# Joining the first feed-forward block and attention of a macaron layer into one program, with batch 0's norm, weight split and projections inside the last feed-forward group

## The reference, cut to what matters

```python
x = x + 0.5 * ffn(layernorm(x), w_gate, w_up, w_down)      # x: (8, 512, 512) float32
x = x + attention(layernorm(x), w_q, w_kv, w_proj, b_proj)
x = x + 0.5 * ffn(layernorm(x), w_gate, w_up, w_down)
# ffn: h = silu(x @ w_gate) * (x @ w_up)   (2048 wide); of each 4 neighbours of h the two of largest
#      size are kept, the others set to 0; then h @ w_down
# attention: 16 heads of 32; one k and one v head shared by all; rotary with xpos scales on q and k;
#      causal softmax; @ w_proj.T + b_proj
```

## Time and profile before

| | us |
|---|---|
| median of 3 runs | 2837.68 |
| lowest, highest | 2837.28, 2841.86 |
| the profiled execution, its own time | 2843.29 |
| its span in the trace | 2841.4 |
| TensorE busy over the span | 2738.1 (96%) |
| VectorE, ScalarE, GpSimd busy | 1863.3, 1127.3, 284.3 |
| mean granted TensorE clock | 0.984 |

### The profile page before, as it was taken

One profiled execution on the slowest core, in us unless ns is written; L12 is line 12 of the kernel. 1 busy time (PEld: TensorE's weight loads), 2 busy tenths in 40 slices (PEclk: granted clock), 3 DMA queues, 4 the chain that ended last, 5 costly groups with the idle time before them and its releaser, 6 DMA issues. The chain is left out here.

```text
span 2841.4 us, 41676 instructions
## 1 busy us (share of the span) xinstructions
PE 2738.1 (96%) x15520; PEld 2198.9 (77%) x15520; DVE 1863.3 (66%) x3543; ACT 1127.3 (40%) x2400; POOL 284.3 (10%) x295
## 2 busy tenths in 40 slices
PE   7999999999999996899999997999999999999998
PEld 6888888888888884567777765888888888888887
DVE  5667656766676655777777765656766766676655
ACT  3323333323333321677777773332333333333331
POOL 0000000000000002344444421000000000000000
PEclk9999999999999997899999998999999999999999
DMA  3210311121121103000000003211121122203100
GB/s 118 98 51 21 128 45 44 61 89 45 45 78 63 48 4 119 1 9 31 28 28 31 16 16 123 85 45 45 60 89 49 48 79 82 68 17 104 45 15 30
DMA packets 65165, 156.48 MB, mean 55 GB/s; under 512 B 6881, under 2 KB 7137, under 8 KB 64737
## 3 DMA queue, kind: packets, MB, share of 16 engines
q1 hardware_dynamic: 64992, 154.17, 16.1%
HBM read 128.97 MB, written 25.17 MB: 54 GB/s over the span
## 5 line engine op out<-in xcount | busy, mean ns | idle before, releaser
L347 PE MATMUL bank<-xnt_h,wgu_h 128*128 128x512 f32 x2048 | 804.0, 393 | 10.3 <-issue 7.4
L347 PE MATMUL bank<-xnt_h,wgu_l 128*128 128x512 f32 x2048 | 799.4, 390 | 0.0
L347 PE MATMUL bank<-xnt_l,wgu_h 128*128 128x512 f32 x2048 | 799.3, 390 | 0.0
L504 DVE TENSOR_TENSOR h<-bank,sg 128x512 f32<-128x512 f32 x256 | 176.9, 691 | 601.4 <-PE bank L347 587.1
L347 PEld LDWEIGHTS bank<-xnt_h,wgu_h 128*128 128x128 f32 x2048 | 385.9, 188 | 91.8 <-issue 8.9
L347 PEld LDWEIGHTS bank<-xnt_h,wgu_l 128*128 128x128 f32 x2048 | 385.8, 188 | 80.7
L347 PEld LDWEIGHTS bank<-xnt_l,wgu_h 128*128 128x128 f32 x2048 | 386.0, 188 | 79.2
L443 ACT ACTIVATE mag<-h 128x512 f32<-128x512 f32 x256 | 162.2, 634 | 702.5 <-DVE h L504 702.5
L366 PE MATMUL bank<-wd_h,hs_h 128*128 128x512 f32 x1024 | 400.5, 391 | 9.1 <-DVE hs_l L539 9.1
L366 PE MATMUL bank<-wd_l,hs_h 128*128 128x512 f32 x1024 | 399.9, 390 | 0.0
L366 PE MATMUL bank<-wd_h,hs_l 128*128 128x512 f32 x1024 | 399.8, 390 | 0.0
(11 more groups left out here) (107 smaller groups left out, 3060.6 us busy)
## 6 DMA issues: line engine op xcount, KB each, us to landing
raw_gu<-in_w_gu SPq DMA_DIRECT2D x128, 512.0 KB, 4.9
raw_d<-in_w_d SPq DMA_DIRECT2D x128, 256.0 KB, 2.6
x_mid<-x_sb SPq DMA_DIRECT2D x64, 256.0 KB, 2.0
x_sb<-in_x SPq DMA_DIRECT2D x32, 256.0 KB, 4.9
x_sb<-x_mid SPq DMA_DIRECT2D x8, 1024.0 KB, 5.7
x_sb<-x_mid SPq DMA_DIRECT2D x32, 256.0 KB, 4.6
out<-x_sb SPq DMA_DIRECT2D x32, 256.0 KB, 2.1
probs<-in_w_q SPq DMA_DIRECT2D x1, 1024.0 KB, 5.4
```

Of the source, the lines that this page charges most:

```text
L347: last = pe.matmul(ps, w[:, r, kind, k], xs[:, b, k], start=(i == 0), stop=(i == 3 * KD - 1))
L504: v.tensor_tensor(h[:, r], bank[UP + r % 2][:, :], sg[:, r % 2], ALU.mult).then_inc(h_done, 1)
```

## The change

What was the feed-forward's block 0 and attention's block become one block. Each engine's program is the feed-forward's, with attention's prologue called in at marked places (`next(then)` runs it to its next `yield`), then the rest of attention.

- Tiles of attention are placed over feed-forward tiles that are read for the last time early enough: `wkv`, `wq`, `kvt`, `kvtok`, `qtmp`, `kt` over the gate and up weights; rotary tables, bias and the raw q and kv weights over `raw_gu`; `raw_p` over `raw_d`; `causal` over `sg`; `qt` over `h`; `probs` and `wp_h` over `hs`.
- In the last group, batch 0 of attention is normalised and transposed between the rows of `gate_up(nn + 1, 1)`, as in the other groups.
- PE runs `project_kv(0)`, four `project_q(0, hg)` and `turn_kv(0)` between `down(nn, 0)` and `down(nn + 1, 1)`, and `turn_k(0)` after the second of the four tiles of the latter. They use the banks 0 to 3.
- The split of weights (copy and subtract) moves from ACT and DVE to POOL (`cut_weights`); `w_p`'s is cut in four and done at units 4 and 8 of attention. POOL's first one waits for the last `gate_up`.
- DVE's part of the prologue (`split_q`, statistics of batch 1, `keys`) comes after `cut_hidden` and ahead of the last four adds (L491).
- Weights are asked for by SP before the last chunk's end; batches 0 and 1 at the last group's start.
- The order at the head of attention changes: `scores`, `turn_x`, `exps`, `mask_scores` as below. The barrier between the two phases is gone; that before the second feed-forward stays.

```diff
@@ ffn_phase, tensor: the end of the last group
-                        if last:
+                    if last and then is None:
                             gate_up(nn + 1, 1, end)
...
                     gate_up(nn + 1, 1, end, lambda r: [turn_first(t) for t in AFTER[r]])
                     down(nn, 0, end, turned=(m + NB) * TT)
+                    if last:
+                        next(then)
+                        down(nn + 1, 1, end, between=lambda t: next(then) if t == 1 else None)
@@ ffn_phase, vector: the end of the last group
                     cut_hidden(nn + 1, 1)
+                    if last:
+                        next(then)
+                        add_down(nn + 1, 1, par)
@@ attention, sync
-                    sp.dma_start(raw_kv, w_kv).then_inc(aw_loaded[0], 16)
...
+                load(0)
+                load(1)
+                yield
+                sp.wait_ge(wgu_done, CHUNKS * NR)
+                sp.dma_start(raw_kv[:, :, :], w_kv).then_inc(aw_loaded[0], 16)
+                sp.dma_start(raw_q[:, :, :], w_q).then_inc(aw_loaded[1], 16)
...
+                sp.wait_ge(wd_done, CHUNKS * NR)
+                sp.dma_start(raw_p[:, :, :], w_p).then_inc(aw_loaded[3], 16)
+                yield
@@ attention, gpsimd
+                def cut_weights(load, h_of, l_of, raw, cut):
+
+                    g.wait_ge(aw_loaded[load], 16)
+                    g.tensor_copy(h_of, raw).then_inc(aw_h_done, 1)
+                    g.wait_ge(aw_h_done, cut)
+                    g.tensor_tensor(l_of, raw, h_of.bitcast(F32), ALU.subtract).then_inc(aw_done, 1)
...
+                    if K in CUT_P:
+                        for c in CUT_P[K]:
+                            cut_weights(3, wp_h[:, c], wp_l[:, c], raw_p[:, c], 2 + KD + c)
...
+                g.wait_ge(up_done, LAST * NR)
+                cut_weights(0, wkv_h[:, :, :], wkv_l[:, :, :], raw_kv[:, :, :], 1)
+                for k in range(KD):
+                    cut_weights(1, wq_h[:, k], wq_l[:, k], raw_q[:, k], 2 + k)
...
+                finish_q(0, 0)
+                finish_q(0, 1)
                 ln_gpsimd(g, m0 + 1, 0)
+                finish_q(0, 2)
+                finish_q(0, 3)
@@ attention, tensor
-                    for t in range(TT):
-                        turn_x(0, t)
-                    pe.wait_ge(aw_done, 1 + KD)
+                pe.wait_ge(aw_done, 1)
                 project_kv(0)
+                pe.wait_ge(aw_done, 1 + KD)
+                for hg in range(NHG):
+                    if hg == NHG - 1:
+                        pe.wait_ge(kvt_done, 1)
+                    project_q(0, hg)
+                pe.wait_ge(q_split, 2)
                 turn_kv(0)
+                yield
+                pe.wait_ge(q_split, 4)
                 turn_k(0)
+                yield
+                pe.wait_ge(q_split, NHG * 2)
+                scores(0)
+                turn_x(1, 0)
+                turn_x(1, 1)
+                scores(1)
+                turn_x(1, 2)
+                turn_x(1, 3)
+                scores(2)
```

More of the change, by code:

```diff
@@ L100, in macaron_kernel, with over @@
     ffn_end = at[0]
-    at[0] = shared_end
+    def over(start, end):
+        assert at[0] <= end, (at[0], end)
+        at[0] = start
+    at[0] = gu_at
+    wkv_h = place("wkv_h", [P, KD, 2 * HD], F32R)
+    wkv_l = place("wkv_l", [P, KD, 2 * HD], F32R)
     wq_h = place("wq_h", [P, KD, D], F32R)
     wq_l = place("wq_l", [P, KD, D], F32R)
[L105 to L108, removed]
+    kvt = place("kvt", [2 * HD, S], F32)
+    kvtok = place("kvtok", [P, 2, TT, 2, HD], F32)
+    xt_raw_at = at[0]
+    kwide = place("kwide", [P, TT, HG, HD], F32)
+    at[0] = xt_raw_at
+    xt_raw = place("xt_raw", [P, KD, P], F32)
+    qtmp = place("qtmp", [P, 2, S], F32)
+    kt = place("kt", [P, 2, S], F32)
+    over(d_at, d_at)
+    pt = place("pt", [P, 2, TT, HG, P], F32)
+    over(raw_gu_at, raw_gu_at)
     rot_q = place("rot_q", [P, 2, S], F32)
@@ L591, in group @@
+                    ln_aggregate(v, m + NB, 0)
+                    step(nn, 0, end, False, True, par)
+                    ln_normalise(v, m + NB, 0, 0, x_next(0, 0))
+                    ln_normalise(v, m + NB, 0, 1, x_next(0, 1))
+                    if not last:
                         for t in range(TT):
@@ L634, in _, with first_block @@
-                    group(0, 0, False, first=True)
-                    with v.Fori(1, GROUPS - 1) as g:
-                        group(g, g % 2, False)
-                    group(GROUPS - 1, (GROUPS - 1) % 2, True)
+                    def first_block(r):
+                        for t in AFTER[r]:
+                            ln_lo(v, m + NB, 0, t, bank[DOWN + t])
+                            if t + 2 < TT:
+                                ln_normalise(v, m + NB, 0, t + 2, x_next(0, t + 2))
+                        if not last and AFTER[r] and AFTER[r][-1] == TT - 1:
+                            ln_normalise(v, m + NB + 1, 1, 0, x_next(1, 0))
+                            ln_normalise(v, m + NB + 1, 1, 1, x_next(1, 1))
@@ new lines, in group @@
+                    hidden(nn + 1, 1, end, not last, first_block)
+                    if not last:
+                        cut_gu(end + 1, NR - 1)
+                    prune(nn + 1)
+                    add_down(nn, 0, par)
+                    cut_hidden(nn + 1, 1)
+                    if last:
+                        next(then)
+                        add_down(nn + 1, 1, par)
+                if phase == 0:
+                    v.sem_inc(h_done, 2)
+                    v.sem_inc(hs_done, NR)
+                    v.sem_inc(added, TT)
@@ new lines, in first_stat @@
+                def first_stat(b, t):
+                    v.wait_ge(x_loaded[b * TT + t], g0 * 16 + 16)
+                    ln_stat_tile(v, b, t, x_sb[:, 0, b * TT + t])
+                for t in range(TT):
+                    first_stat(0, t)
+                ln_aggregate(v, m0, 0)
+                for t in range(TT + 1):
+                    if t < TT:
+                        ln_normalise(v, m0, 0, t, x_sb[:, 0, t])
+                    if t >= 1:
+                        ln_lo(v, m0, 0, t - 1, bank[DOWN + t - 1])
+                        first_stat(1, t - 1)
@@ L644, in attention_phase @@
+                ln_aggregate(v, m0 + 1, 1)
+                for r in range(NR):
+                    cut_gu(c0, r)
+                    if r < 2:
+                        ln_normalise(v, m0 + 1, 1, r, x_sb[:, 0, TT + r])
+                group(0, 0, False, first=True)
+                with v.Fori(1, GROUPS - 1) as g:
+                    group(g, g % 2, False)
+                group(GROUPS - 1, (GROUPS - 1) % 2, True)
+            return sync, gpsimd, tensor, scalar, vector
         def attention_phase(src, dst, m0):
```

1565 lines of the change are left out of this document (770 added, 795 removed).

## The result

The changed kernel takes 2806.02 us (median of 4 runs, 2805.92 to 2810.18), the kernel before 2837.48 beside it (4 runs, 2836.03 to 2841.86): a ratio of 0.9888, interval 0.9874 to 0.9902, 31.5 us less where 27.6 were forecast. Measured twice more on other occasions the ratio was 0.9890 and 0.9883. The span of the profiled execution is 2804.1, against 2841.4.

The account below looks back on a forecast made before the run. TensorE's idle time between the phases was what could be had: 38.3 + 0.9 (weights) + 8.8 (keys) + 2.4 (clock) + 10.5 (tail) = 60.9 us for 88.5, 27.6 less, so 2810.1 us; range 2799 to 2819, forecast band 2804 to 2816 (0.60).

Parts of the forecast that it names:

- rival A: Pruning beside GpSimd's weight split: no turns at the port, no wait for weights; 39.7 us less, 2798; chance 0.17.
- the signs named in the prediction: TensorE gaps: none before last down, some 1 us before wq, 5 to 12 at kwide; longer pruning; second feed-forward unchanged.
- Where the time is: Stretch from last group's first down(nn, 0) matmul to batch 1's project_kv: 88.5 us, only place of gain, to become 60.9.
- The port: VectorE and GpSimd wait for each other's whole instructions; the weight split makes the pruning some 7 us longer than 9.1.
- each as waiting for the other: Eight GpSimd and eight VectorE instructions alternate in the pruning: split ends about 1078.4, hs_l at 1086.4, 7 us later.
- Keys: TensorE waits 8.8 us for kwide in the middle of the last down, as keys ends only at 1104.1.
- The clock: Behind the kwide gap the clock is low: ten matmuls cost 2.0 us more and the turn 0.4, together 2.4.
- The tail: From the last down to batch 1's project_kv, a ladder between ScalarE and VectorE: 10.5 us, before 17.
- Rival B: Tail keeps its 17 us, or keys comes 6 later: 2817; with w_p's 7.6 coming through, 2824; chance 0.18.
- Costs at nothing: DMAs, SP's waits, batch 0's statistics and w_p's split at units 4 and 8 (at worst 7.6 us) put at zero.
- Rival C: Slower than before: GpSimd's queue stretched by VectorE, some 20 instructions by 2.0 us each, 40 us late; chance 0.02.
- No other stage's matmuls are changed: The saving lies wholly in the one stretch; the second feed-forward must take as long as before.

Follow-up runs that it names:

- experiment 2: Changed kernel with GpSimd's first split of weights waiting for the end of the pruning instead of the last gate_up; 2812.64 us, ratio 0.9898.
- experiment 8: Changed kernel with GpSimd's split of the wq weights done twice, nothing left out; 2819.14 us, ratio 0.9927 to the kernel before.
- experiment 1: Changed kernel with VectorE's keys(0) moved ahead of split_q(0, 2), the two normalisations and split_q(0, 3); 2801.3 us, ratio 0.9861.
- experiment 5: experiment 1 plus a scratch exponential on ScalarE ahead of drain_k(0), loading the table early; 2796.89 us, ratio 0.9842.
- experiment 6: experiment 5 plus batch 1's second hi_x ahead of the first exponentials on ScalarE; 2799.96 us, ratio 0.9850; again 2798.93, 0.9854.
- experiment 4: Changed kernel with the five rounded copies of wkv and wq on ScalarE, GpSimd keeping the subtracts; 2804.65 us, ratio 0.9875.
- experiment 3: Changed kernel with the old seam order: last down whole before the projections, VectorE's last adds ahead of its prologue part; 2821.75 us, ratio 0.9933.
- experiment 7: experiment 6 plus the five rounded copies of wkv and wq on ScalarE, as in experiment 4; 2797.1 us, ratio 0.9851.

## Why the prediction was right

2806 lies 2 us above the border of rival A, so the time alone would not decide for the mechanism; the signs named in the prediction do. The last `down` did not wait, `kwide` waited 8.09 us for VectorE, GpSimd's instructions and the pruning were longer, and the clock was low behind the wait. Two signs failed: the gap of some 1 us ahead of `wq` was not there, and the second feed-forward was 2.1 us shorter.

**Where the time is.** All that the forecast counted on came from the stretch, and the matmuls in it cost what the rows of the second feed-forward said: 24.61 us for 108 matmuls against 24.5.

**The port.** Right in kind, and the decisive choice between the forecast and rival A: experiments 2 and 8 take the meeting away and lengthen it, and the pruning goes to 9.15 and 17.5 from 14.75. By the rule of the Trainium skill (SBUF — State Buffer, "Who interferes with whom"), a GpSimd instruction that only writes is no rival, and the traces agree as far as they go: the fill of `causal` took 0.53 while VectorE's `kdif` ran, and 0.53 in the kernel before. The size was somewhat too high: 7 us of lengthening, 5.6 measured. The step "each as waiting for the other" counted eight full turns; that part of each fell while the other engine was between instructions is likely, and was not tested by itself. The split ended at 1076.89 instead of 1078.4, so the wait of 0.9 for `wq` was not there.

**Keys.** The wait of 8.8 was 8.09, with its cause, the order on VectorE and `rstd` behind two `finish_q`, as forecast; experiment 1 shows that another order takes all of it away. That the number came so close is partly luck. `hs_l` came 1.5 earlier and TensorE reached the wait 0.7 earlier; and in VectorE's chain between, the two normalisations took 2.84 instead of 3.5, but `keys` 4.4 instead of 3.5, since `kwide` itself also shared the port (1.37 instead of 0.43).

**The clock.** 2.4 was put for the half clock after that gap, from the ten slow matmuls behind a shorter gap (4.00 us is their distance from first to last, nine steps; the ten steps took 4.38, so 2.1 more than at full clock). In the profiled execution only the turn and the five matmuls behind it ran slow, 7.35 - 6.0 = 1.35 us in sum, and by this trace it is the term of the sum that was furthest off. But the same kernel's second and third traces give 1.4 and 2.5 (7.44 and 8.50 us): the term is one that differs between executions, and the forecast's size lies in its range.

**The tail.** 10.5, measured 10.11, and experiments 5 and 6 remove two of its links one at a time, 1.2 and 1.7 us. Rival B wanted 17 here, or `keys` some 6 us later, and `keys` ended at 1102.4 where 1104.1 was forecast: both are excluded.

**Costs at nothing.** The split of `w_p` at units 4 and 8 came to nothing: TensorE's gaps in batch 0 are the same in both kernels (0.52, 2.6 or 2.3, 1.53, 0.33, 1.36 us), and none is released by GpSimd. Rival C needed 27.6 us of lateness at GpSimd; its longest instruction in the stretch was 2.15.

**What was outside.** "No other stage's matmuls are changed" holds, but their time moved: 6.9 us of the profiled difference lie there. The saving is 3.9 larger than forecast, of which the stretch's terms give 2.9 in the profiled execution, and 1.7 in the third one, where the clock cost more; the rest is of the size by which those other phases differ between executions.

## What to carry to other kernels

Fill a wait at a seam with work that is ready, and then ask what is last in its queue: here the projections covered `hs_l`, and the wait moved to `keys`, which stood behind a norm that nobody wanted yet. Weight preparation on GpSimd beside two-input VectorE work costs both engines, but it is cheap where TensorE has work in hand, and dear right in front of its consumer. Cost such an overlap by rows where both were at work, and count a turn for each instruction of the longer queue, less something for the gaps between (here 5.6 us where eight full turns were put at 7; with half of GpSimd's instructions gone still 4.8).

## What the runs showed of the hardware that was not expected

How many matmuls run at half clock (starts 0.43 apart instead of 0.23) after an idle stretch is not fixed by the code. After 8.09 us of idling five of `down`'s ran so in the changed kernel. The third time, with the same instructions and 8.10 us of idling, ten did:

```profile
1101.63 1.08 PE L935 MATMUL bank<-ident,kwide 128*128 128x128 f32 x4 [8.10 <-DVE kwide L1184]
...
1106.36 0.62 PE L387 MATMUL bank<-wd_h,hs_h 128*128 128x512 f32 x1
...
1110.13 0.50 PE L967 MATMUL bank<-kt,qt 32*128 32x128 f32 x8
```

The row at 1106.36 is the tenth. From the turn to `scores(0)` this took 8.50 us instead of 7.35, which is the whole difference of the two stretches, 57.46 and 56.30. At the head of the second feed-forward, the same instructions in each kernel, the granted clock of the first 7 us was:

```profile
1733.39:1740.39 7.00, 7.00 (x24) 5.64 (x25) 4.41 (x5) 2.60 (x3) 1.04 (x1) 0.75 0.57 180
```

for the changed kernel, and, with the kernel before and then experiment 6,

```profile
1768.61:1775.61 7.00, 7.00 (x18) 5.51 (x19) 4.41 (x5) 2.59 (x3) 1.04 (x1) 0.56 0.64 182
```

```profile
1720.48:1727.48 7.00, 7.00 (x19) 5.52 (x20) 4.40 (x5) 2.60 (x3) 1.04 (x1) 0.57 0.58 186
```

24 matmuls started in it, or 18 and 19. This phase took 1070.2 to 1071.1 us in the changed kernel, all three times, and experiments 1, 2, 4 and 8, and 1072.1 to 1072.8 in the kernel before and 3, 5, 6, both times, and 7. Experiments 3 and 7 had the quick head, 25 and 24 matmuls, but 14 matmuls at half clock behind the last gap of the phase, where the changed kernel had 6 or 7. Batch 0 is the same case. In the changed kernel it took 69.36 at a clock of 0.98, and the third time, with the same instructions and waits of TensorE that differ by at most 0.2 us,

```profile
1120.24:1191.46 71.22, 64.76 (x678) 45.74 (x677) 51.34 (x179) 53.60 (x163) 34.55 (x36) 0.95 0.01 2
```

So the 3.1 us that batch 0 was shorter than in the kernel before are not shown to be the change's. The second feed-forward came out the same each time that a kernel was traced again, the changed one short in three traces and experiment 6 long in two; whether the shorter stretch has any part in which of the two comes is open: no run varied it alone. For a change of 0.1% in this kernel the traced stretch, read with its clock, tells more than the median does.
